# Two row transforms of a convolution stack with their odd halves at half the columns, and mirrored samples added and subtracted on GpSimd and VectorE

## The reference

```
X = jnp.fft.rfftn(x, axes=(-2, -1), norm='backward')
Xr, Xi = (jnp.real(X), jnp.imag(X))
...
Yr = _rconv(Xr, wr) - _rconv(Xi, wi) + b_real[:, None, None]
Yi = _rconv(Xr, wi) + _rconv(Xi, wr) + b_imag[:, None, None]
Y = lax.complex(Yr, Yi)
return jnp.fft.irfftn(Y, axes=(-2, -1), norm='backward')
```

## Time and profile before

| what | value |
|---|---|
| device time, median of 3 runs | 6531.92 us (6527.77 to 6534.83) |
| span of the profiled execution | 6537.8 us |
| PE busy | 5657.3 us, 87% |
| DVE busy | 4850.6 us, 74% |
| ACT busy | 4524.3 us, 69% |
| POOL busy | 2728.2 us, 42% |

### The profile page before, as it was taken

How to read it: one execution, slowest core, us unless ns; L and a number is a source line. 1 busy time by engine, 2 the same in 40 slices (tenths; PEclk the granted TensorE clock), 3 DMA queues, 4 the chain that set the end, 5 groups by cost and what they waited for, 6 DMA issues and landing times. The chain is left out here.

```text
span 6537.8 us, 200097 instructions
## 1 busy us (share of the span) xinstructions
PE 5657.3 (87%) x63882; PEld 3655.6 (56%) x63882; DVE 4850.6 (74%) x9636; ACT 4524.3 (69%) x8793; POOL 2728.2 (42%) x4634
## 2 busy tenths in 40 slices
PE   0289979979979989988988997995988989889889
PEld 0057748748747757756766775872433434334334
DVE  5778877877887887887887887767766667667664
ACT  2577767767766766767766556657877877778776
POOL 3165555656656556546646556650111111111112
PEclk9899989989999999999999999998999999999999
DMA  6516616615624633642651551553766767667665
GB/s 199 154 57 186 184 42 189 184 58 174 184 84 145 184 116 115 185 144 87 185 166 49 142 141 36 157 151 74 205 164 168 194 168 198 166 166 201 161 163 138
DMA packets 535620, 959.14 MB, mean 147 GB/s; under 512 B 121946, under 2 KB 126682, under 8 KB 532826
## 3 DMA queue, kind: packets, MB, share of 16 engines
q1 hardware_dynamic: 467546, 799.21, 44.2%
q10 hardware_dynamic: 67456, 151.01, 7.3%
HBM read 560.66 MB, written 287.60 MB: 130 GB/s over the span
## 5 line engine op out<-in xcount | busy, mean ns | idle before, releaser
L1635 PE MATMUL pC<-xs,taps 128*128 128x512 f16 x4608 | 1094.6, 382 | 107.7 <-DMA xhalo<-xs 100.6
L964 PE MATMUL pM<-gw,xh 64*128 64x256 f16 (+1 forms) x24960 | 1128.2, 244 | 0.0
L964 PEld LDWEIGHTS pM<-gw,xh 64*128 64x128 f16 x24960 | 966.8, 95 | 129.2 <-issue 3.3
L726 POOL TENSOR_TENSOR X<-X,zo 128x256 f32 (+1 forms) x512 | 371.2, 725 | 1218.1 <-DVE X L1084 1218.1
L1635 PEld LDWEIGHTS pC<-xs,taps 128*128 128x128 f16 x4608 | 448.7, 98 | 670.8 <-DVE xs L1685 89.9
L1531 POOL TENSOR_TENSOR xn<-xn,one_col 128x1 f32<-128x1 f32 x520 | 172.3, 331 | 1409.7 <-ACT xn L1565 1409.7
L1551 ACT ACTIVATE scaled<-X,qbias,qscale 128x512 f32 (+1 forms) x512 | 411.4, 804 | 335.4 <-DMA X<-after_layer 306.0
L272 PE MATMUL pM<-X,mix0s 64*64 64x512 f32 x2304 | 523.3, 624 | 136.7 <-DVE X L1056 108.6
L1084 DVE SCALAR_TENSOR_TENSOR X<-pZ,X 128x512 f32 (+1 forms) x512 | 354.1, 692 | 340.8 <-ACT zo L785 339.6
L1573 ACT ACTIVATE xs<-xn 128x1028 f16<-128x1028 f32 x520 | 545.7, 1049 | 87.5 <-POOL xn L1532 86.5
L711 POOL TENSOR_TENSOR X<-X,rl 128x512 f32 x384 | 478.3, 1276 | 267.5 <-ACT rl L756 267.3
(11 more groups left out here) (241 smaller groups left out, 13574.5 us busy)
## 6 DMA issues: line engine op xcount, KB each, us to landing
gw<-row_weights SPq DMA_DIRECT2D x520, 288.0 KB, 3.3
after_layer<-X SPq DMA_DIRECT2D x512, 256.0 KB
out_dram<-result SPq DMA_DIRECT2D x512, 256.0 KB
X<-in_x_dram SPq DMA_DIRECT2D x448, 256.0 KB
X<-after_layer ACTq DMA_DIRECT2D x224, 512.0 KB, 5.9
stage<-in_x_dram SPq DMA_DIRECT2D x192, 512.0 KB
xhalo<-xs SPq DMA_DIRECT2D x504, 96.4 KB, 3.6
qhalo<-q SPq DMA_DIRECT2D x496, 96.2 KB, 4.0
```

Of the source, the lines that this page charges most:

```text
L726: nc.gpsimd.tensor_tensor(X[:, j, 0], X[:, j, 0], zo[:, k], ALU.add)
L964: nc.tensor.matmul(pY[:, r, col:col + nd * P], row(xh, r)[:, k, p, ri, off:off + P], weights(r, q_, d, nd, ri), start=ri == 0 and off == 1 ...
L1635: nc.tensor.matmul(bank, taps3[:, d, wh], xs[:, h, own, d:d + W], start=d == 0 and n == 0, stop=False)
```

## The change

The odd frequencies of a row depend on the 256 differences of samples half a row apart. Before, those 256 values are multiplied by a table of 256 samples by 256 results (128 cosines and 128 sines). After, mirrored differences are folded first: the sums of value n+1 and value 256-n-1 carry the sines, the differences of value n and value 256-n the cosines, 128 each, and each of the two groups is multiplied by a table of 128 by 128. The inverse transform does the same the other way round: PE makes 128 cosine parts and 128 sine parts, and their sums and differences are the 256 odd values.

So the 6 matmuls with `fwd_odd` and the 6 with `inv_odd` have 128 columns in place of 256; their number stays. POOL's `folded` has six additions in place of four (two more, 128 wide, two of the operands read backwards), with a one-buffer tile `dif` and two more semaphores. DVE gets two additions of 129 and 127 columns for each tile, both from SBUF (`zs`, which ACT now writes), the second one read backwards; POOL's `odd_part` waits for them (`odd_ready`) and no longer for `z_free`. To make room `unused` becomes one buffer, and half of ACT's squares write to `rhi`.

```
-    t["fwd_odd"] = fwd(2 * np.arange(NO) + 1, HALF)
+    n, k = np.arange(NO)[:, None], 2 * np.arange(NO)[None, :] + 1
+    m = np.stack([np.cos(2 * np.pi * ((n * k) % W) / W),
+                  -np.sin(2 * np.pi * (((n + 1) * k) % W) / W) * np.where(n + 1 == NO, 0.5, 1.0)], 1) * F_SCALE
...
-            fwd_odd = sb("fwd_odd", [P, 2, 2, 2 * NO], f16, p1)
+            fwd_odd = sb("fwd_odd", [P, 2, 2, NO], f16, p1)
...
-            inv_odd = sb("inv_odd", [P, 2, 2, HALF], f16, p1)
+            inv_odd = sb("inv_odd", [P, 2, 2, NO], f16, p1)
...
                     def folded(b, i, k):
                         pool.wait_ge(xn_ready, b * ITEMS + i + 1)
+                        pool.wait_ge(dif_free, b * ITEMS + i + 1)
+                        nc.gpsimd.tensor_tensor(dif[:, 0:HALF], xn[:, k, 0:HALF], xn[:, k, HALF:W], ALU.subtract).then_inc(dif_done, 1)
                         nc.gpsimd.tensor_tensor(even[:, k], xn[:, k, 0:HALF], xn[:, k, HALF:W], ALU.add).then_inc(even_done, 1)
-                        nc.gpsimd.tensor_tensor(fold[:, k, HALF:W], xn[:, k, 0:HALF], xn[:, k, HALF:W], ALU.subtract)
+                        pool.wait_ge(dif_done, b * ITEMS + i + 1)
+                        nc.gpsimd.tensor_tensor(fold[:, k, HALF:HALF + NO], dif[:, 0:NO], dif[:, HALF:NO:-1], ALU.subtract)
+                        nc.gpsimd.tensor_tensor(fold[:, k, HALF + NO:W], dif[:, 1:NO + 1], dif[:, HALF - 1:NO - 1:-1], ALU.add).then_inc(dif_free, 1)
                         pool.wait_ge(even_done, b * ITEMS + i + 1)
...
                     def odd_part(b, i, k):
 
                         j = i - 1
-                        pool.wait_ge(z_free, b * ITEMS + i + 1)
+                        pool.wait_ge(odd_ready, b * J + i)
...
-                            nc.scalar.activation(zo[:, k], pZ[:, HALF:W], ACT.Copy,
+                            nc.scalar.activation(zs[:, k].rearrange("p (t n) -> p t n", t=2)[:, :, 0:NO],
+                                                 pZ[:, HALF:W].rearrange("p (t n) -> p t n", t=2), ACT.Copy,
...
-                                three(pF[:, 0, 0:2 * NO], lambda h, c=n + 2: xt[:, o, h, c * P:(c + 1) * P],
+                                three(pF[:, 0, n * NO:(n + 1) * NO], lambda h, c=n + 2: xt[:, o, h, c * P:(c + 1) * P],
...
-                                three(pZ[:, HALF:W], lambda h, c=c: yt[:, o, h, c * P:(c + 1) * P],
+                                three(pZ[:, HALF + c * NO:HALF + (c + 1) * NO], lambda h, c=c: yt[:, o, h, c * P:(c + 1) * P],
...
                                                            accum_out=sum2[:, bass.ds(j, 1)]).then_inc(z_free, 1)
+                            nc.vector.tensor_tensor(zo[:, k, 0:NO + 1], zs[:, k, 0:NO + 1], zs[:, k, NO + 1:HALF + 2], ALU.add)
+                            nc.vector.tensor_tensor(zo[:, k, NO + 1:HALF], zs[:, k, HALF:NO + 1:-1], zs[:, k, NO - 1:0:-1],
+                                                    ALU.subtract).then_inc(odd_ready, 1)
```

More of the change, by code:

```diff
@@ L85, in tables @@
     t["fwd_2"][..., NO // 2::NO // 2 + 1] = 0
-    t["fwd_odd"] = fwd(2 * np.arange(NO) + 1, HALF)
+    n, k = np.arange(NO)[:, None], 2 * np.arange(NO)[None, :] + 1
+    m = np.stack([np.cos(2 * np.pi * ((n * k) % W) / W),
+                  -np.sin(2 * np.pi * (((n + 1) * k) % W) / W) * np.where(n + 1 == NO, 0.5, 1.0)], 1) * F_SCALE
+    m[np.abs(m) < 1e-9] = 0
+    t["fwd_odd"] = np.stack(halves(m), 2)
     n2 = np.arange(HALF)
@@ L98, in tables @@
     t["inv_even"] = inv(2 * np.arange(NO))
-    t["inv_odd"] = inv(2 * np.arange(NO) + 1)
+    k, n = 2 * np.arange(NO)[:, None] + 1, np.arange(NO)[None, :]
+    m = np.stack([np.cos(2 * np.pi * ((k * n) % W) / W), -np.sin(2 * np.pi * ((k * (n + 1)) % W) / W)], 1) * (2.0 / W * I_SCALE)
+    m[np.abs(m) < 1e-9] = 0
+    t["inv_odd"] = np.stack(halves(m), 2)
     full = np.arange(W)
@@ L550, in program @@
                 rl = sb("rl", [P, 4, W], f32, pm)
-                unused = sb("unused", [P, 2, W], mybir.dt.bfloat16, pm)
+                unused = sb("unused", [P, W], mybir.dt.bfloat16, pm)
                 tmax = sb("tmax", [P, J], f32, pm)
@@ L573, in program @@
                 even = sb("even", [P, 2, HALF], f32, pm)
+                dif = sb("dif", [P, HALF + 1], f32, pm)
                 stats_1 = even[:, 0, 0:3 * J].rearrange("p (g k s) -> p g k s", k=2, s=6)
                 zo = sb("zo", [P, 2, HALF], f32, pm)
+                zs = sb("zs", [P, 2, HALF + 4], f32, pm)
                 es = zo[:, :].rearrange("p k w -> p (k w)")
@@ L600, in program @@
                 yt_done, yt_hi, yt_lo = s_("yt_done"), s_("yt_hi"), s_("yt_lo")
-                zo_ready, x2_ready, sq2_done = s_("zo_ready"), s_("x2_ready"), s_("sq2_done")
+                zo_ready, x2_ready, sq2_done, odd_ready = s_("zo_ready"), s_("x2_ready"), s_("sq2_done"), s_("odd_ready")
                 z_done, z_free, edge_hi, edge_ready = s_("z_done"), s_("z_free"), s_("edge_hi"), s_("edge_ready")
-                even_done = s_("even_done")
+                even_done, dif_done, dif_free = s_("even_done"), s_("dif_done"), s_("dif_free")
                 tile_stats = s_("tile_stats")
@@ L700, in _ @@
                 def _(pool):
+                    nc.gpsimd.memset(dif[:, HALF:HALF + 1], 0.0)
+                    nc.gpsimd.memset(zs[:, :, :], 0.0)
                     nc.gpsimd.memset(xh[:, :, :, :, :], 0.0).then_inc(pads_ready, 1)
                     pool.wait_ge(pads_ready, 1)
+                    pool.sem_inc(dif_free, 1)
                     def root(b, n):
@@ L762, in squares @@
                         act.wait_ge(sq_done, b * (J // 4 * 2) + g * 2 + k + 1)
-                        nc.scalar.activation(unused[:, k], Xf[:, g * 4 + k], ACT.Square, bias=shift[:, :],
+                        nc.scalar.activation((unused, rhi)[k][:, :], Xf[:, g * 4 + k], ACT.Square, bias=shift[:, :],
                                              accum_out=sq1[:, k, bass.ds(g, 1)]).then_inc(sq_done, 1)
@@ L790, in squares2 @@
                         act.wait_ge(x2_ready, b * J + j + 1)
-                        act.wait_ge(sq2_done, b * J + j - 1 + 4)
-                        nc.scalar.activation(unused[:, k % 2], Xf[:, j], ACT.Square, bias=mean_1[:, 1:2],
+                        act.wait_ge(sq2_done, b * J + j + 4)
+                        nc.scalar.activation(unused[:, :], Xf[:, j], ACT.Square, bias=mean_1[:, 1:2],
                                              accum_out=sq2[:, bass.ds(j, 1)]).then_inc(sq2_done, 1)
```

## The result

The changed kernel takes 6225.5 us (median of 4 runs, 6217.3 to 6232.1), the kernel before 6530.2 (4 runs, 6527.8 to 6534.8): a ratio of 0.9532, with a 95% interval of 0.9517 to 0.9547. That is 305 us less; 303 were forecast.

The account below looks back on a forecast made before the run. PE was taken as the bound: 61 steps x 0.624 = 38.1 us, + 0.8 - 0.4 = 38.5 per image, x 8 = 308, minus 5 for the last image: 303 saved, 6229 us; range for 8 in 10, 6205 to 6350.

Parts of the forecast that it names:

- PE's saving: In each pipeline step, twelve matmuls narrowed to 128 columns save 0.052 us each on PE, 0.62 us per step.
- DVE covered: DVE's two additions per step cost 0.20 us each; two steps need 10.5 us against PE's 10.95.
- rival 1: DVE's additions wait 0.25 us each for POOL instructions, making DVE the bound: 166 us saved, 6366 us; chance 20%.
- Its time at half that delay: DVE's additions each wait half of 0.25 us for POOL; the kernel was put at 6290 us.
- the 5 us of the last image: In the last image's steps without pairs, POOL may be level with PE, losing 0.08 us on 60 steps.
- rival 3: Weight loads set the pace of PE's 128-column matmuls, about 81 ns each: 170 us saved, 6362 us; chance 6%.
- rival 2: Backward reads and waits bring POOL's step to 5.7 us, making POOL the bound: 195 us saved, 6337 us; chance 6%.
- rivals 4 and 5: Steady steps: DVE additions waiting for whole POOL instructions give 6795 us (4%); additions at 0.6 us eat the gain (2%).
- Start and end: Per image, the start up to L983 gains 0.8 us and DVE's additions add 0.4 us at the end.

## Why the prediction was right, point by point

**PE's saving: right, a hair small.** I took 0.110 - 0.058 = 0.052 per matmul and 0.624 us per step. The steps went from 12.19 to 10.91 us for two, 0.640 each, so a matmul of 128 columns costs 0.056 from start to start where I took the 0.058 of the 130-column row. The steps of an image fell from 367.76 us to 329.05 in the undisturbed ones (38.7) and by 38.1 in the mean over the first seven images. That the mean meets the 38.1 forecast is luck in part: 488 steps at 0.640 in place of 0.624 would give 8 us more; the first step of each image saves only half (5.80 us became 5.48), which takes 3 us, and longer steps take 4.

**Why the mean is less.** Some 18 steps of images 0 to 4 are longer than the same steps of images 5 and 6, by 4.4 us in all. The longest one, with ACT, DVE and PE in it:

```profile
1074.48 0.39 PE L1000 MATMUL pZ<-edge_back,back 128*128 128x512 f16 x1
...
1076.23 1.06 ACT L816 ACTIVATE unused_x<-stage 128x1024 bf16<-128x1024 f32 x1 [2.31 <-DMA stage<-in_x_dram]
...
1077.29 0.58 ACT L853 ACTIVATE yt<-pM 128x512 f16<-128x512 f32 x1
...
1077.90 0.69 DVE L1141 TENSOR_TENSOR yt<-pM,yt 128x512 f16<-128x512 f32 x1 [1.41 <-ACT yt L853]
...
1078.73 2.16 PE L981 MATMUL pM<-gw,xh 64*128 64x256 f16 x48 [0.59 <-DVE yt L1141]
...
1081.18 0.39 PE L1000 MATMUL pZ<-edge_back,back 128*128 128x512 f16 x1
```

ACT stood 2.31 us for a load into `stage`, so the high half of `yt` (L853) came late, DVE's half waited 1.41 us for it, and PE 0.59 for DVE. The step, from 1074.48 to 1081.18, took 6.70 us in place of 6.04. From 440 to 4050 us ACT waits for such a load 34 times here, 39.5 us in all, and once, 0.4 us, in the kernel before, which took 367.76 or 367.77 us for the 61 steps of each of the first seven images. So with the longer steps the loads came in time. That it is the shorter step that brings this out was read from the traces alone; no kernel with another buffer for `stage` was run. Nor is it all: the step from 1525.78 us on takes 5.80 us in place of 4.87, and in it PE stands 0.77 us among the 64-row products (L989) for nothing that the profile shows. The cause of that one stays open.

**DVE covered: right.** The additions cost 0.20 us each from start to start, as forecast. In every second step they lie in the gap ahead of `xt`; in the others they are followed by `ymin` at once, and DVE's slack takes them. The slack was given as 0.45 us per two steps and is 0.53, since the chain is 10.38, not 10.5. The kernel with one reduction more bears this out: its two steps take the 11.04 us of the sum.

**The port (rival 1): right to leave out, and real.** It takes 0.34 us from the addition that meets a POOL instruction. In the changed kernel the additions start when POOL has run dry, as the prediction argued, so it hardly shows in images 0 to 6: of the 448 first and the 448 second additions 21 each last over 0.4 us. The kernel with the additions moved shows what it costs where they meet, together with the empty gap: 93 us. Rival 1 took 0.25 for every addition; here it was 0.34, for one addition in two steps. (Its time at half that delay is mis-added: four additions of 0.325 us give 11.0 us for two steps, 0.59 saved per step and some 6240 us, not 6290.)

**POOL: covered, and the 5 us of the last image were wrong.** The forecast took 0.08 us off each of its 60 steps. Its 61 steps take 297.59 us, 4.869 from start to start apart from the first and last few, and 297.53 in the kernel without the mirrored additions. A window and two timelines of that image, POOL and DVE:

```profile
3850.00:4000.00 150.00, 150.00 (x2933) 131.68 (x2930) 137.36 (x308) 108.55 (x248) 137.81 (x247) 1.00 0.67 178
```

```profile
3903.40 0.45 POOL L735 TENSOR_TENSOR rl<-even 128x128 f32<-128x128 f32 x1
3904.40 0.73 POOL L742 TENSOR_TENSOR X<-X,zo 128x256 f32 x1 [0.55 <-DVE zo L1105]
```

```profile
3903.41 0.59 DVE L1104 TENSOR_TENSOR zo<-zs 128x129 f32<-128x129 f32 x1
3903.92 0.28 DVE L1105 TENSOR_TENSOR zo<-zs 128x127 f32<-128x127 f32 x1
```

POOL works 137.81 of 150 us, 4.47 of every 4.87, and waits the rest for DVE. It is nearly full but not the limit. Here DVE's first addition does meet L735 and lasts 0.59, but with no pair in the step DVE has the time: it waited 0.53 us for `zs` just before.

**Weight loads (rival 3): did not happen.** 128 columns cost 0.056 us, under the 81 ns of the Trainium skill ("TensorE: Matmul & The Clock Gate", Back-to-back issue gap), so the measurement decides against the figure in this stream. **POOL as the bound (rival 2)** did not happen: it needed more than the 0.96 us by which the kernel with more work on POOL lengthens POOL's step. There POOL sets the pace in the last image and is only level with PE in the steps with pairs. **Slower, or no change (rivals 4 and 5)** needed some 0.6 us per addition in every step with pairs. The additions moved on DVE came to 0.54 for one in four. Only with POOL never idle did they reach that price, 0.55 and 0.74 us, and that in the steps without pairs, where DVE is not the bound.

**Start and end.** PE waits 7.11 us for the first fold in place of 6.28: 0.83 more, 0.82 forecast. From that first transpose to the first L1000 it takes 21.60 us in the mean of the eight images, where it was 22.55. The start as a whole gains 0.95 - 0.82 = 0.13 us where I gave it 0.8: here the size was off, though within its bounds. The forward groups gave what was forecast: the first two take 0.64 and 0.62 us for 1.28 and 1.26, at a granted clock of 0.50 in both kernels. What was undersized is what PE waits in between: from the first transposes of image 0 to its first L1000 3.61 us (1.90 and 0.61 for POOL, 0.24 and 0.86 for DVE) in place of 2.73. At the end, the two steps up to the 64th gain 0.36 us as a rule and what is behind them loses 0.74: 0.4 net, as forecast.

**The sum.** By stages the 307.6 us between the two spans are 305.2 in the 8 x 61 steps, 1.0 at the starts, -4.0 at the ends, and 5 in the parts that the change doesn't touch (the time ahead of the first image, the stretch between two images, the last part); one such stretch, ahead of the pipeline, took 84.9 to 86.4 us within this one execution. The forecast of 303 was 305 + 6 - 3 - 5. It has two errors that cancel: 5 us for POOL in the last image, which were not lost, and 5 too many gained at the starts. So the mechanism was right and most terms are met, but that the touched stages give 302 us for a forecast of 303 is in part luck, and so is the 305 of the medians, where parts that the change doesn't touch vary by as much.

## What to carry over

Before work is moved to a less busy engine, sum that engine's chain from start to start over a whole period and compare it with the period of the engine that sets the pace; here 10.38 stood against 10.91 us, and the same sum told the pace with one instruction more on that engine (11.04 us). Then look for where on the engine the work goes: the same two additions cost next to nothing in a gap where the other engine was idle too, and 93 us a few instructions later. Stretches with a shorter period than the steady one (the steps ahead of the first pair, the last image) need a sum of their own.

## What the runs showed of the hardware that was not expected

- An addition on DVE with both operands in SBUF that starts while POOL is in its folds lasts 0.61 us in place of 0.28, and the POOL instruction keeps its 0.45. With POOL never idle, the second addition of a step was 514 ns in the mean.
- Which engine gives way is not fixed: before the change POOL's addition was the one stretched, to 0.90 us, and some of its folds still are (903 ns at most).
- Reading operands in falling order made no difference that the kernel's time shows: DVE's addition with two of them took 286 ns for 283 forwards, one of POOL's folds 455 for 451, and the folds that always read forwards 456 and 457. One fold fell from 457 to 413 ns with the forward read, for a reason not shown.
- A matmul of 128 columns with its own load of 128 x 128 weights costs 0.056 us from start to start, about half of the 0.109 with 256 columns.
